# Two transformer layers on one core: GpSimd subtractions in halves, the first 512 positions projected and stacked first, residual rows by a second load, the next projection ahead of the last downs

## The reference

```
xn = layernorm(x)
x  = x + attention(xn) + (silu(xn @ Wg.T) * (xn @ Wu.T)) @ Wd.T
```

## Time and profile before

| | us |
|---|---|
| median of 3 runs | 2059.18 (2049.17 to 2060.20) |
| the profiled execution | 2055.59 |
| its span, first to last instruction | 2053.8 |
| TensorE busy | 1866.4 |
| VectorE, ScalarE, GpSimd busy | 1116.6, 1060.1, 703.4 |
| mean granted TensorE clock | 0.958 of full speed |

### The profile page before, as it was taken

One profiled execution on the slowest core, in us unless ns is written; L12 is line 12 of the kernel. 1 busy time (PEld: TensorE's weight loads), 2 busy tenths in 40 slices (PEclk: granted clock), 3 DMA queues, 4 the chain that ended last, 5 costly groups with the idle time before them and its releaser, 6 DMA issues.

```text
span 2053.8 us, 25605 instructions
## 1 busy us (share of the span) xinstructions
PE 1866.4 (91%) x8656; PEld 1347.6 (66%) x8656; DVE 1116.6 (54%) x2432; ACT 1060.1 (52%) x2353; POOL 703.4 (34%) x516
## 2 busy tenths in 40 slices
PE   4999999999899899898889999999988998998987
PEld 3777767775675666656467777776757756575654
DVE  6554647373755564736346465573746636455452
ACT  2464646556256473646425646464652555646363
POOL 3225243242341533333213243534314415233320
PEclk9999999999999899999779999999999999999989
DMA  4213113031130313103213131311401403121201
GB/s 159 67 42 98 42 44 90 27 99 41 52 88 22 87 47 73 42 21 109 72 62 78 37 92 42 84 56 29 122 11 52 101 9 98 42 68 37 66 7 41
DMA packets 59874, 126.20 MB, mean 61 GB/s; under 512 B 9440, under 2 KB 10464, under 8 KB 58720
## 3 DMA queue, kind: packets, MB, share of 16 engines
q1 hardware_dynamic: 59744, 124.57, 22.0%
HBM read 69.48 MB, written 4.19 MB: 36 GB/s over the span
## 4 chain that ended last, share of the span: by engine, by line
PE 69%; DVE 11%; ACT 6%; SPq 5%; issue 5%; POOL 3%; DMA 2%; DVEq 0%; ACTq 0%; POOLq 0%
PE D L905 15%; PE G L905 11%; PE U L905 8%; PE OE L999 7%; PE SS L983 6%; PE OE L905 6%; PE SS L905 6%; SPq L564 5%; PE OE L983 3%; PE OE L962 3%; PE SS L962 2%; DVE OE L826 2%; ACT OE L618 2%; ACT pr L634 2%; DMA QS<-pr 1%
## 5 line engine op out<-in xcount | busy, mean ns | idle before, releaser
L874 DVE TENSOR_TENSOR xres<-D,xres 128x512 f32<-128x512 f32 x352 | 243.1, 691 | 214.1 <-PE D L905 209.7
L634 ACT ACTIVATE pr<-SS 128x512 f32<-128x512 f32 (+3 forms) x512 | 232.2, 501 | 143.8 <-PE SS L983 135.5
L709 POOL TENSOR_TENSOR hl<-tt,hh 128x512 fp32r<-128x512 f32 x108 | 139.0, 1287 | 475.7 <-ACT hh L651 475.7
L618 ACT ACTIVATE OE<-OE,mp 128x384 f32<-128x384 f32 (+3 forms) x256 | 203.4, 795 | 104.9 <-DVE mp L826 104.0
L826 DVE CUSTOM_DVE_ANT_0 OE<-OE,mask 128x384 f32<-128x384 f32 (+3 forms) x256 | 220.5, 873 | 50.6 <-PE OE L962 49.7
L618 ACT ACTIVATE SS<-SS,mp 128x128 f32<-128x128 f32 (+3 forms) x256 | 162.2, 634 | 95.7 <-DVE mp L826 94.0
L728 POOL TENSOR_SCALAR_AFFINE_SELECT pr<-pr 128x512 f32<-128x512 f32 x128 | 81.0, 635 | 378.7 <-ACT pr L634 378.7
L826 DVE CUSTOM_DVE_ANT_0 SS<-SS,mask 128x128 f32<-128x128 f32 (+3 forms) x256 | 167.6, 673 | 64.3 <-PE SS L962 63.0
L905 PE MATMUL G<-xh,wgh 128*128 128x512 f32 x432 | 178.0, 412 | 24.0 <-DVE tt L885 22.8
L983 PE MATMUL SS<-QS,KS 98*128 98x512 f32 (+2 forms) x512 | 182.1, 413 | 14.9 <-ACT pr L634 12.3
L905 PE MATMUL D<-wdh,hh 128*128 128x512 f32 x432 | 174.2, 403 | 19.6 <-DVE xres L874 13.7
(11 more groups left out here) (123 smaller groups left out, 3733.6 us busy)
## 6 DMA issues: line engine op xcount, KB each, us to landing
KS<-pr SPq DMA_DIRECT2D x192, 128.0 KB, 2.3
QS<-pr SPq DMA_DIRECT2D x192, 128.0 KB, 2.3
raw<-in_wgate_dram SPq DMA_DIRECT2D x27, 512.0 KB, 3.7
raw<-in_wup_dram SPq DMA_DIRECT2D x27, 512.0 KB, 3.7
raw<-in_wdown_dram SPq DMA_DIRECT2D x27, 512.0 KB, 3.7
raw<-in_wqk_dram SPq DMA_DIRECT2D x16, 512.0 KB, 4.4
val<-in_x_dram SPq DMA_DIRECT2D x4, 1024.0 KB, 6.9
trig<-in_wv_dram SPq DMA_DIRECT2D x4, 1024.0 KB, 5.6
```

Of the source, the lines that this page charges most:

```text
L618: act.activation(s, s, ACT.Exp, bias=mp[:, c, at:at + 1], scale=-1.0, accum_out=se[:, c, at:at + 1]) \
L634: act.activation(weights(i)[:, h, skip:W], SB[(i * HG + h) % 3][:, skip:W], ACT.Exp, scale=-1.0) \
L709: pool.tensor_tensor(hl[:, fc, :], tt[:, (blk * nfc + fc) % 2, :], hh[:, fc, :].bitcast(F32), ALU.subtract) \
L874: dve.tensor_tensor(xres[:, rt, :], d[:, :], xres[:, rt, :], ALU.add).then_inc(sem["v_dfree"], 1)
```

## The change

- GpSimd's subtractions of 1024 columns (`low`) become two of 512, and that of the value weights, 2048 columns, four of 512.
- `proj` and `rotate` t now mean K and Q of the first 512 positions for t = 0 and 1, and of the second for t = 2 and 3. SP stacks after each of the four: 12 DMAs of 64 KB each time, 48 a turn in place of 24. The first two groups raise `d_stack` of their heads, the last two `d_later`, for all of which nat 16 waits.
- Nat 0 to 3 wait for the release of each projection's bank instead of for all of it.
- `keep` becomes a DMA of SP from the input into `xres`, behind the store's landing; ScalarE's copy goes. The first add into each row block waits for it (`d_keep`). Adds no longer wait for the add just before, only for one into the same row block; ScalarE's waits in `st` and `gated` stand once a set and once a pair.
- `v_weights` moves behind the first two norms. At a join `proj` 0 and `values` 0 of the next layer go ahead of the last four downs, and the last turn's `wo` right behind its `heads`. The opening's order changes with it.
- `guess` leaves VectorE: ScalarE does the linear step itself, ahead of its exponential.
- Gate and up are cut into three pieces of four matmuls instead of two of six, and every string of `PACE` is new.

```diff
-GU_PARTS = 2
+GU_PARTS = 3
...
     n = len(SETS)
-    items.append([("pv", n - 2), ("pv", n - 1), ("heads", 1)])
+    items += [[("pv", n - 2), ("pv", n - 1), ("heads", 1)] + [("x_next",)] * (l == 1 and not final)] + output(1)
...
-        pieces += rows + g1[GU_PARTS:] + output(1) + [piece + [("row", 1, TPC + i)] for i, piece in enumerate(d1)]
+        pieces += rows + g1[3:] + early(1) + [piece + [("row", 1, TPC + i)] for i, piece in enumerate(d1)]
         items += norms(1, range(TPC))
+        items[-3].append(("v_weights", 1))
...
+def early(layer):
+
+    return [[("proj", 0, True)], [("values", 0, layer)]]
 
 
 def normal(layer):
 
-    return [("stats", layer, 0)] + [("v_weights", 1)] * layer + [("xn", layer, 0), ("xn", layer, 1)]
+    return [("stats", layer, 0), ("xn", layer, 0), ("xn", layer, 1)]
...
+    out += [("stats", layer, 1), ("xn", layer, TPC), ("xn", layer, TPC + 1), proj[0], values[0], values[1], ("rotate", 0)]
+    out += values[2:4] + later[0] + [proj[1]] + later[1] + later[2] + later[3] + [("keep", 1)] * (layer == 0) + [values[4]]
+    return out + [*values[5:], ("rotate", 1), proj[2], ("rotate", 2), proj[3], ("rotate", 3)]
...
-         "00700010101001100112021102021111111020010020010000100100000100100001000010010000010010001001000000000",
+         "00300021010200020102021212121211111020110100202000100010000100100000000010010000010010000012000000000",
...
+            def keep(n, c):
+                sp.wait_ge(sem["d_out"], n("d_out"))
+                sp.dma_start(xres[:, c * TPC:(c + 1) * TPC, :], rows(x, n, c, n.batches)).then_inc(sem[f"d_keep{c}"], 16)
...
             def rotate(n, t):
-                if t % NC < NC - 1:
-                    return
-                qk = t // NC
+                qk, c = t % 2, t // 2
+                cols = slice(c * W, (c + 1) * W)
                 flats = ((flat_h, flat_h, flat_l), (flat_h, flat_l, flat_h))[qk]
                 sp.wait_ge(sem["g_rl"], n("g_rl", 1))
                 if qk:
                     sp.wait_ge(sem["p_v"], n("p_v"))
                 for h in range(HG):
+                    done = sem["d_later" if c else f"d_stack{h}"]
                     for r, src in enumerate(flats):
                         at = slice(r * DH, (r + 1) * DH)
-                        sp.dma_start((QS[at, :, h, :] if qk else KS[at, h, :]).bitcast(F32),
-                                     src[qk][h * DH:(h + 1) * DH, :]).then_inc(sem[f"d_stack{h}"], 16)
+                        sp.dma_start((QS[at, c, h, :] if qk else KS[at, h, cols]).bitcast(F32),
+                                     src[qk][h * DH:(h + 1) * DH, cols]).then_inc(done, 16)
...
-            def keep(n, c):
-                act.wait_ge(sem[f"d_x{c}"], n(f"d_x{c}", 16))
-                act.wait_ge(sem["d_out"], n("d_out"))
-                act.copy(xres[:, c * TPC:(c + 1) * TPC, :], val[:, c * TPC:(c + 1) * TPC, :]) \
-                    .then_inc(sem["a_keep"], 1)
...
             def guess(n, c):
-                act.wait_ge(sem["v_lse"], n("v_lse", 2))
+                act.wait_ge(sem["a_nat"], n("a_nat"))
+                act.activation(y0[:, :], se[:, c, :].bitcast(I32), ACT.Copy, scale=LN2 / 2 ** 23, bias=-(127 - 0.043) * LN2).then_inc(sem["a_log"], 1)
+                act.wait_ge(sem["a_log"], n("a_log", 1))
                 act.activation(ex[:, :], y0[:, :], ACT.Exp, scale=-1.0).then_inc(sem["a_log"], 1)
...
             def low(kind, src):
                 hi, lo = SPLIT_TO[kind]
-                return pool.tensor_tensor(flat(lo), src[:, 0:SIZE[kind]], flat(hi).bitcast(F32), ALU.subtract)
+                for at in range(0, SIZE[kind], W):
+                    part = slice(at, at + W)
+                    ins = pool.tensor_tensor(flat(lo)[:, part], src[:, part], flat(hi)[:, part].bitcast(F32), ALU.subtract)
+                return ins
...
             def add(n, done, rt):
-                dve.wait_ge(sem["v_dfree"], n("v_dfree"))
+                if n.fresh(rt):
+                    dve.wait_ge(sem[f"d_keep{rt // TPC}"], n(f"d_keep{rt // TPC}"))
+                if n.close(rt):
+                    dve.wait_ge(sem["v_dfree"], n("v_dfree"))
                 dve.wait_ge(sem[done], n(done))
...
                 elif t == HG * TPC:
+                    pe.wait_ge(sem["d_later"], n("d_later"))
                     pe.wait_ge(sem["a_nat"], n("a_nat", -2))
```

More of the change, by code:

```diff
@@ L229, in opening @@
 def opening(layer):
-    out = []
-    proj = [("proj", t) for t in range(2 * NC)]
-    values = [("values", rt) for rt in range(RT)]
+    proj = [("proj", t, True) for t in range(2 * NC)]
+    values = [("values", rt, layer) for rt in range(RT)]
     later = norms(layer, range(TPC, RT))
-    out += [("row", 0, rt) for rt in range(TPC, RT) if layer == 0]
-    out += [("stats", layer, 1), ("xn", layer, TPC), ("xn", layer, TPC + 1), proj[0], values[0], values[1]] + later[0] + [values[2]]
-    out += later[1] + [values[3]]
@@ L247, in opening @@
-    return out
-START = [("row", 0, rt) for rt in range(TPC)] + [("stats", 0, 0), ("v_weights", 0), ("xn", 0, 0), ("xn", 0, 1)]
-START += [x for piece in norms(0, range(TPC)) for x in piece] + [("keep", 0)]
+    out = [("row", 0, rt) for rt in range(TPC, RT) if layer == 0]
+    out += [("stats", layer, 1), ("xn", layer, TPC), ("xn", layer, TPC + 1), proj[0], values[0], values[1], ("rotate", 0)]
+    out += values[2:4] + later[0] + [proj[1]] + later[1] + later[2] + later[3] + [("keep", 1)] * (layer == 0) + [values[4]]
@@ L282 @@
     "stats": {"v_chain": 13},
[L283 removed]
+    "keep": {},
     "x_next": {"d_x0": 16, "d_x1": 16},
```

149 lines of the change are left out of this document (81 added, 68 removed).

## The result

The changed kernel takes 2167.1 us (median of 4 runs, 2164.69 to 2167.37) beside 2057.7 us of the kernel before (2049.17 to 2060.20): ratio 1.0537, 95% interval 1.0505 to 1.0569, so 110 us more. The profiled execution took 2167.37 us, its span is 2165.6 us against 2053.8. The forecast was 2109 us with a range of 2018 to 2138; slower was right, the size was not: 53 us more were forecast, 110 came.

A forecast was written before the change was run, and what follows sets the result against it. TensorE was taken as the bound in general, elsewhere a chain across other engines. Terms 77 + 6 - 18 + 9 + 8 - 29 - 8 + 8 = +53 on the profiled 2055.6 us gave 2109 us, range 2018 to 2138.

The forecast's parts named there:

- SP's price: Stack issues on SP: a 64 KB transfer takes 0.63 us to issue, so 48 take 30.2 us.
- Layer 0's inner turns: Six inner turns of layer 0, up to nat 16: 15.7 us idle instead of 2.9, +77 us.
- First turns: Layer 0's two first turns: nat 16 comes 19.6 us after the projections instead of 21.9, idle 6.2 for 3.1, +6 us.
- Clock and natural scores: TensorE at half clock after six long stalls in layer 0, half absorbed by slack: +8 us, bounds 0 to 30.
- Layer 1: Layer 1's turns, where latency counts: later nat 16 and longer weights stages against shorter natural stages, together +8 us.
- 77 + 6 - 18 + 9 + 8 + 8: Layer 0's inner turns, first turns, last turns' weights, other weights stages; then layer 1; then the clock, in us.
- Sum -29: Start and joins of layers and batches: v_weights behind the norms, second load, early projection; -29 us, bounds 0 to -45.
- Together -8: GpSimd's halved subtractions, guess moved to ScalarE and dropped waits: -8 us in all, bounds 0 to -25.
- rival 2: All 16 turns: the wait comes, but finer pieces and shorter GpSimd instructions save 4 us more each; 2045 us, chance 0.13.
- The 12 us between the batches: Join of the batches: a second load takes the residual copy off ACT, and proj 0 and values 0 move earlier; 12 us saved.
- Halves: GpSimd's subtractions in halves: some 18 us more on GpSimd, on no path, and shorter VectorE waits behind them; within the -8.
- Guess: Guess replaces two 16-element VectorE instructions, 32 times, by one small ACT instruction; within the -8 us.

The follow-up runs named there:

- e1: The kernel before with each of its 24 stack transfers a turn cut into two of 64 KB, nothing else changed; 2245.64 us, ratio 1.0938.
- e5: The changed kernel with added matmuls that nobody reads, put where TensorE waits for the stacks; 2157.84 us, ratio 1.0481.
- e3: The changed kernel with the 12 transfers of Q's first 512 positions issued by ScalarE's queue instead of SP's; 2098.30 us, ratio 1.0228.
- e10: The changed kernel with projections in the order K, K, Q, Q, 24 transfers of 128 KB and old digits, other parts kept; 2074.86 us, ratio 1.0098.
- e13: The kernel before with gate and up in three pieces instead of two, digits for the same work ahead of every item; 2077.78 us, ratio 1.0104.
- e16: The kernel before with v_weights behind the first two norms at the start and the joins, nothing else changed; 2041.51 us, ratio 0.9926.
- e6: The changed kernel with v_weights back ahead of the first two norms; 2169.29 us, ratio 1.0540.
- e7: The changed kernel with proj 0 and values 0 of the next layer back in the opening, behind the last downs; 2188.20 us, ratio 1.0629.
- e18: The kernel before with guess on ScalarE, ScalarE's two waits dropped, v_weights late, residual rows by a second load and fewer add waits; 2021.23 us, ratio 0.9846.
- e8: The changed kernel with GpSimd's subtractions, those of the value weights too, in one instruction again; 2168.79 us, ratio 1.0539.
- e15: The kernel before with guess on ScalarE alone and ScalarE's waits in st and gated dropped; 2039.12 us, ratio 0.9910.
- e14: The kernel before with proj 0 and values 0 of the next layer ahead of the last four downs; 2062.96 us, ratio 1.0031.

## Why the prediction was partly right

**SP's price: right.** 0.63 us an issue was taken, and 48 took 31.0 us. Nat 16 was put 29.6 us behind the projections in inner turns; by the same marks it came at 29.6 to 30.8. The Trainium skill, "DMA: Bandwidth & Descriptors", "Issuing engines are not separate DMA queues", calls the time in which a sequencer starts a DMA usually small beside the DMA. The trace disagrees: 0.59 us for 64 KB against a landing at 2.0, with the DMA engines 0.43 busy, and e1 pays 193 us for 24 issues more a turn.

**Layer 0's inner turns: right.** Idle time of the first stage +81.4 us (100.6 after, 19.2 before), forecast +77. Nat 0 came at 8.6 to 8.7 us, 8.8 by the forecast.

**First turns: 10.7 us short.** Forecast 19.6 us to nat 16, measured 21.4 to 22.3, and the idle time of layer 0's two rises by 16.7 us instead of 6. About half of that is the step "Q0 starts when the values end, ahead of the last two projections (5.4 us)". The opening after the first layer, by ScalarE, GpSimd and SP; the projections end at 634.6:

```profile
629.19 0.59 ACT L622 COPY val<-OE 128x512 f32<-128x512 f32 x1 [2.13 <-PE OE L926]
629.67 0.62 ACT L630 CAST pr<-pr 128x512 fp32r<-128x512 f32 x1
```
```profile
630.37 1.29 POOL L748 TENSOR_TENSOR pr<-pr 128x512 fp32r<-128x512 f32 x1 [14.74 <-ACT pr L630]
```
```profile
631.68 4.30 SPq L590 DMA_DIRECT2D QS<-pr  x7
```

Rotate 1 stands behind values 7 in the list, so Q0's high part is made only behind the last values' copy on ScalarE: SP starts 2.9 us ahead of the projections' end, not 5.4. The other half, 5 us, is a wrong count of the kernel before. The "13.4 us of work instead of 18.8" leaves out the last value projection, 12 matmuls or 2.7 us, that followed there on the last projection:

```profile
69.68 0.61 PE L905 MATMUL OE<-QS,xh 128*128 128x512 f32 x2
```

With it 21.3 to 21.5 of the 21.9 us were work, and the first turn had about 0.5 us idle, not 3.1.

**Clock and natural scores: under-sized.** +8 was forecast; the natural scores of layer 0 alone lose 18.2 us. e5 shows 11 us, 18 in the natural scores, for two thirds of the extra slow matmuls, e3 shows 31 us won in both layers' natural scores once nat 16 is on time.

**Layer 1: 10 us short in time** (+18.1 for the stages up to the last exponential, forecast +8). Inner turns up to nat 16 +22.8 (forecast +20), first turns -1.4 (forecast -5), natural scores -8.5 (-20), weights +5.2 (+13), each from start to start. The floor of 34 us for a natural stage wasn't reached behind a late nat 16. Besides, 5.4 us of value projections had moved out of these stages into the openings, which the comparison in time left out.

Taken together, though, stacks and digits were well sized: the terms 77 + 6 - 18 + 9 + 8 + 8 give +90, and e10 against the changed kernel shows 90. That is in part chance: by stages they came higher, and parts of the other group lie in the same stages.

**The step that failed is the rest: "Sum -29" for the joins and "Together -8" for halves and guess, where e10 shows +20.** Those 57 us are the whole gap between +53 and +110. Four causes:

- *Finer pieces had no term at all*; they appear only in rival 2, as a gain. Alone, with the rounding of the digits that came with them, they cost 21 us (e13). Against rival 2 this is the sign that was wrong.
- *Joins*: idle time fell by 27.7 us in the tails and 3.3 at the start, near the 29, but the new openings give 13.7 back. I had worked the tails and not followed the rest. v_weights behind the norms is worth its 15 alone (e16: 3.9 at the start, 10.1 in the tails) and nothing measurable in the changed kernel (e6). The likely reason is VectorE's wait for the rotary table (20.2 us in four openings, above), which comes only where both parts meet: there is none in e6, 1.8 us in e7 and 2.0 in e16. The 12 us between the batches were put down to ScalarE's copy; e18 shows that it wasn't the copy.
- *Halves*: 0 (e8). The xn pair ran in 1.01 us at 579.54 in the changed kernel, where v_weights had been moved away, against 5.18 before, but e8 shows no time gained by the halves themselves. The Trainium skill, "SBUF — State Buffer", "Who interferes with whom", says that whichever of VectorE and GpSimd takes their shared ports first keeps them for its whole instruction and blocks the other; the 5.18 us beside a subtraction of 4.73 agree with it.
- *Guess*: worth 18 us (e15 with ScalarE's waits), forecast inside the -8. I priced the instructions (16 elements) and not the wait in front of them.

Alone the four parts sum to 21 + 6 - 18 - 15 = -6 us (the second load would add some -4), and e10 has +20. The 26 us between lie in its openings, where idle time rises by 24.4 us (15.7 in e14), and ahead of nat 0 in the four first turns, 16.2 us against 0.9. The new order of the opening was not run alone, so this stays open; e10 also moves proj 1 in it.

Of what was to show it: 768 issues near 0.6 us came; the waits at nat 16 came, 4.8 to 9.3 us in all 16 turns where 8 to 12 in twelve were said; half clock behind them came; layer 0's last turns were full (2.4 and 1.3 us idle).

## What to carry to other kernels

Where a queue issues at a fixed price, a transfer cut in two for an earlier start is paid by the last one: count issues up to the last that anyone waits for, and put work there. When a planner's units and order change, give the finer cut and the new order a term of their own. And price a tiny instruction by the idle time in front of it in its queue: here one of 0.18 us had 35.7 us of it in 30 waits, and the kernel without it in that queue (and without two of ScalarE's waits) took 18 us less. Not tried here were the new order of the opening by itself, a third queue for the last twelve transfers, and fewer but larger transfers.

## What the runs showed of the hardware

- An issue of a stack transfer takes SP 0.59 us at 64 and at 128 KB, one of 8 KB 0.58, and ScalarE's queue takes about the same: 12 in 7.82 us (64 KB) and 12 in 7.80 us (128 KB). It isn't one price for every transfer: SP issues most weight loads of 512 KB in 0.37 us, as the line below shows (the changed kernel). With 64 KB the DMA engines are 0.43 busy (104 GB/s), with 128 KB 0.89.
- ScalarE executed nothing while it issued: 7.36 us ahead of its next copy in e3. With gate pieces as cover this reached TensorE as a wait of 11.77 us.
- Behind a wait of 4.45 us the granted clock was 0.55 for 3.2 us, behind 9.28 us 0.50 for 5.8 us; with 18 matmuls in the wait and 0.38 us left of it, it stayed 1.00.

```profile
L517 SPq DMA_DIRECT2D raw<-in_wgate_dram x27: 367/368/3932, 8.1 to 1988.9; - x27
```
